# First layer of a hybrid block: the output product of six groups laid out with channels on the partitions and fed in split parts

## The reference, cut to what matters

```python
DIM, H, P, N = (256, 32, 64, 128)         # x: [1, 1024, 256]
proj = x @ Win.T                           # x_ssm, z: H*P each; B, C: H*N each; dt: H
dt = softplus(dt_raw + dt_bias)
xc, Bc, Cc = (silu(causal_conv(u, w)) for ...)     # 4 taps, per channel
decay = exp(dt * -exp(A_log)); dtx = dt[..., None] * xc
def step(h, inp):                          # one state of 64 x 128 for each head, zero at the start
    h = dec_t[..., None, None] * h + dtx_t[..., None] * B_t[:, :, None, :]
    y = jnp.einsum('bhpn,bhn->bhp', h, C_t)
y = y * rsqrt(mean(y * y, axis=-1) + 1e-06)        # norm over the 64 channels of a head
y = y * silu(z)
return y.reshape(B, T, H * P) @ Wout.T     # [1024, 2048] x [2048, 256]
```

## Time and profile before

| | us |
|---|---|
| median of 3 runs (1118.32 to 1120.6) | 1119.31 |
| the profiled execution | 1119.11 |
| its span, first to last instruction | 1117.8 |
| busy: PE | 1051.8 (94%) |
| busy: DVE | 779.3 (70%) |
| busy: POOL | 656.9 (59%) |
| busy: ACT | 595.8 (53%) |

### The profile page before, as it was taken

How to read it: one execution, slowest core, us unless ns; L and a number is a source line. 1 busy time by engine, 2 the same in 40 slices (tenths; PEclk the granted TensorE clock), 3 DMA queues, 4 the chain that set the end, 5 groups by cost and what they waited for, 6 DMA issues and landing times.

```text
span 1117.8 us, 24089 instructions
## 1 busy us (share of the span) xinstructions
PE 1051.8 (94%) x10046; PEld 875.9 (78%) x10046; DVE 779.3 (70%) x1177; ACT 595.8 (53%) x923; POOL 656.9 (59%) x651
## 2 busy tenths in 40 slices
PE   8899999999999999999989899998888879999998
PEld 6677788888888888888877788887654567788887
DVE  5679887888878888888857545555758853654554
ACT  5886787766677766777615222224954542423221
POOL 3967666677555776557653568554366452175553
PEclk9999999999999999999999999999999989999999
DMA  3322112111112121111200543302121120143321
GB/s 108 109 67 76 48 58 67 47 69 58 63 51 77 39 68 57 48 48 40 57 11 3 190 151 117 100 19 67 43 89 28 32 65 2 56 167 99 118 67 38
DMA packets 47217, 75.97 MB, mean 68 GB/s; under 512 B 11330, under 2 KB 34150, under 8 KB 47110
## 3 DMA queue, kind: packets, MB, share of 16 engines
q1 hardware_dynamic: 47110, 74.44, 20.8%
HBM read 68.13 MB, written 2.36 MB: 63 GB/s over the span
## 4 chain that ended last, share of the span: by engine, by line
PE 65%; DVE 17%; ACT 7%; POOL 5%; issue 4%; DMA 3%; SPq 0%; DVEq 0%; POOLq 0%; ACTq 0%
PE psum L654 33%; PE psum L877 8%; DVE arena L1581 6%; PE psum L742 5%; PE psum L626 4%; PE psum L784 4%; DVE arena L1618 3%; PE psum L734 2%; PE psum L986 2%; ACT arena L1166 1%; PE psum L950 1%; PE psum L1014 1%; DVE arena L1827 1%; DMA vT<-arena 1%; POOL arena L2034 1%
## 5 line engine op out<-in xcount | busy, mean ns | idle before, releaser
L654 PE MATMUL psum<-vT,split 128*128 128x512 f32 x2136 | 539.8, 402 | 12.9 <-DVE arena L1581 5.5
L654 PEld LDWEIGHTS psum<-vT,split 128*128 128x128 f32 x2136 | 391.6, 189 | 103.3 <-DVE arena L1581 7.5
L1581 DVE SCALAR_TENSOR_TENSOR arena<-psum,arena 128x1023 f32<-128x1023 f32 (+2 forms) x208 | 265.3, 1277 | 81.8 <-ACT arena L1166 65.5
L2007 POOL TENSOR_TENSOR split<-arena,split 128x256 fp32r<-128x256 f32 x178 | 132.9, 756 | 85.4 <-ACT split L1091 85.1
L1166 ACT ACTIVATE arena<-psum,arena 128x512 f32<-128x512 f32 x160 | 108.2, 691 | 137.5 <-PE psum L654 137.5
L2187 POOL TENSOR_TENSOR arena<-arena,bcast 128x512 f32<-128x512 f32 x64 | 84.6, 1324 | 113.3 <-ACT arena L1298 95.4
L1298 ACT ACTIVATE arena<-psum,arena 128x512 f32<-128x512 f32 x72 | 49.7, 690 | 173.6 <-PE psum L654 173.6
L1719 DVE SCALAR_TENSOR_TENSOR arena<-psum,arena 128x512 f32<-128x512 f32 x72 | 53.9, 749 | 123.0 <-POOL arena L2187 118.0
L877 PEld LDWEIGHTS psum<-split_down,split_hid 128*128 128x128 f32 x864 | 113.4, 192 | 10.2 <-DVE split_hid L1730 3.6
L877 PE MATMUL psum<-split_down,split_hid 128*128 128x256 f32 x864 | 116.2, 285 | 2.8 <-DVE split_hid L1730 2.8
L2034 POOL TENSOR_TENSOR arena<-arena,v 128x1021 f32<-128x1021 f32 x32 | 76.3, 2385 | 70.5 <-DVE arena L1581 70.5
(11 more groups left out here) (200 smaller groups left out, 1486.1 us busy)
## 6 DMA issues: line engine op xcount, KB each, us to landing
bcast<-scratch_a SPq DMA_DIRECT2D x32, 512.0 KB, 3.8
bcast<-scratch_e SPq DMA_DIRECT2D x32, 512.0 KB, 4.2
arena<-in_w_a SPq DMA_DIRECT2D x16, 768.0 KB, 4.4
arena<-in_wg SPq DMA_DIRECT2D x36, 128.0 KB, 3.6
arena<-in_wu SPq DMA_DIRECT2D x36, 128.0 KB, 3.5
arena<-in_wd SPq DMA_DIRECT2D x36, 128.0 KB, 3.9
arena<-in_wout_a SPq DMA_DIRECT2D x8, 256.0 KB, 4.5
vT<-arena SPq DMA_DIRECT2D x2, 1024.0 KB, 5.1
```

Source lines behind the costliest of these rows:

```text
L654: m = pe.matmul(bank, split[:, t % SPLITS, i, q, :], vT[:, j, q, half * BANK:(half + 1) * BANK], start=(n == 0), stop=(n == 3 * KD - 1))
L1581: dve.scalar_tensor_tensor(out=tile[:, s:T], in0=bank[:, 0:T - s], scalar=cw_a[:, j, i, TAPS - 1 - s:TAPS - s], in1=tile[:, s:T], op0=ALU. ...
L2007: pool.tensor_tensor(split[:, t % SPLITS, 1], raw, split[:, t % SPLITS, 0].bitcast(F32), ALU.subtract).then_inc(sem["split"], 1)
```

## The change

Groups 0 to 5: DVE's `gate` writes one buffer; ACT copies it as hi part (`gated_hi`), POOL subtracts to make the lo part (`gated_lo`), into `split_hid` (even pairs) or `split_gate` (odd pairs); Wout of the group is split in the same way (`wout_hi`, `wout_lo`). A unit of `project_out` is now 128 output channels by 512 tokens: six matmuls with 512 columns, Wout stationary. DVE adds units into `acc_a`, with channels on the partitions. Both late units come in odd pairs j, both early units in even pairs. In pair 15 `acc_a` is transposed back (units A) and added to x. Group 6 is multiplied in split parts after the loop (`last_split_out`, 48 matmuls with 256 columns), group 7 as before. `across` leaves out chunk 0, whose incoming state is zero; POOL sets that part of y to zero (`first_zero`). The last pair's squares, sums and norm go by heads. The buffers for gated y and Wout shrink; `experts` wait for `out_split` before they write `split_down` and `split_hid`.

```diff
+SUMMED = PAIRS // GROUP - 2
-def out_unit(j, late):
-    return [("O", (j - 3) // 2, 2 * (1 - j % 2) + late)] if j >= 3 else []
+def out_early(j):
+    if j == PAIRS - 1:
+        return [("A", 0), ("A", 1)]
+    return [("O", j // 2 - 2, 1, dh) for dh in range(2)] if j >= 4 and j % 2 == 0 else []
+def out_late(j):
+    if j == PAIRS - 1:
+        return [("A", 2), ("A", 3)]
+    return [("O", (j - 3) // 2, 0, dh) for dh in range(2)] if j >= 3 and j % 2 == 1 else []
...
@@ SP
-                        if g >= 2:
-                            on.wait_ge(sem["unit"], N_FILLED["O", g - 2, 3])
-                        load(f"wo{g % 2}", wout_a[:, g % 2], io["wout_a"][g])
+                        if g:
+                            on.wait_ge(sem["wo_lo"], g)
+                        load("wo0", wout_a, io["wout_a"][g])
@@ PE
-                    for c in range(NC):
+                    for c in range(1, NC):
                         m = by_halves(bank[:, c * PA:(c + 1) * PA], chunk(cv_a[:, j % 2, 3 + g, :], c),
...
+                        if unit[0] == "A":
+                            on.wait_ge(sem["dve_done"], N_DVE["O", SUMMED - 1, 1, 1])
+                            cs = (2 * unit[1], 2 * unit[1] + 1)
+                            transposes(unit, [chunk(acc_a[:, dh], c) for c in cs for dh in range(KD)])
+                            continue
+                        _, g, q, dh = unit
+                        on.wait_ge(sem["gated_lo"], GROUP * (g + 1))
+                        on.wait_ge(sem["wo_lo"], g + 1)
+                        for n, (i, (iw, ih)) in enumerate((i, p) for i in range(GROUP) for p in PRODUCTS):
+                            m = pe.matmul(bank, split_down[:, i, iw, dh * P:(dh + 1) * P], gated_parts(i)[:, ih, q],
+                                          start=(n == 0), stop=(n == 3 * GROUP - 1))
...
+                def last_split_out():
+                    on.wait_ge(sem["gated_lo"], GROUP * (SUMMED + 1))
+                    on.wait_ge(sem["wo_lo"], SUMMED + 1)
+                    for i in range(GROUP):
+                        for c in range(NC):
+                            for n, (iw, ih) in enumerate(PRODUCTS):
+                                m = pe.matmul(psum[:, c * D:(c + 1) * D],
+                                              gated_parts(i)[:, ih, c // 4, c % 4 * P:(c % 4 + 1) * P],
+                                              split_down[:, i, iw], ...)
+                    m.then_inc(sem["out_split"], 1)
...
-                    project_out(out_unit(j, 0))
+                    project_out(out_early(j))
...
-                    project_out(out_unit(j, 1))
+                    project_out(out_late(j))
...
-                project_out(out_unit(PAIRS, 0) + out_unit(PAIRS, 1))
+                last_split_out()
+                give_back(PAIRS - 1)
                 last_out(0)
-                give_back(PAIRS - 1)
                 last_out(1)
@@ ACT
+                def gated_hi(j):
+                    on.wait_ge(sem["dve_done"], N_DVE["F", j, 1])
+                    if j >= GROUP:
+                        on.wait_ge(sem["unit"], N_FILLED["O", j // GROUP - 1, 1, 1])
+                    act.copy(gated_parts(j)[:, 0], A["gated"].rearrange("p (q t) -> p q t", q=2)).then_inc(
+                        sem["gated_hi"], 1)
+                def wout_hi(g):
+                    act.copy(split_down[:, 0:GROUP, 0, :], wout_a).then_inc(sem["wo_hi"], 1)
...
                     turned(j, 1, 0)
+                    if j >= 3 and j % 2 == 1:
+                        gated_hi(j - 2)
                     project_to(1)
...
                     turned(j, 1, 1)
+                    if j >= 2 and j % 2 == 0:
+                        gated_hi(j - 2)
+                    if j >= 3 and j % 2 == 1:
+                        wout_hi((j - 3) // 2)
                     project_to(2)
@@ DVE
+                    _, g, q, dh = unit
+                    acc = acc_a[:, dh, q * BANK:(q + 1) * BANK]
                     if g:
+                        dve.tensor_tensor(acc, bank_of(unit), acc, ALU.add).then_inc(sem["dve_done"], 1)
+                    else:
+                        dve.tensor_copy(acc, bank_of(unit)).then_inc(sem["dve_done"], 1)
...
                     across(j, 0)
                     inside(j, 0)
+                    if j == PAIRS - 1:
+                        sum_squares_head(j, 0)
                     taps(4, 1)
-                    add_out(out_unit(j, 1))
+                    add_out(out_late(j))
@@ POOL
+                def first_zero(j):
+                    pool.memset(y_a[:, j % 2, 0, :], 0.0).then_inc(sem["y_zero"], 1)
+                def gated_lo(j):
+                    parts = gated_parts(j)
+                    on.wait_ge(sem["gated_hi"], j + 1)
+                    pool.tensor_tensor(parts[:, 1], A["gated"].rearrange("p (q t) -> p q t", q=2),
+                                       parts[:, 0].bitcast(F32), ALU.subtract).then_inc(sem["gated_lo"], 1)
...
                     carry_u(j, 1)
+                    first_zero(j)
                     project_to(1)
+                    if j >= 3 and j % 2 == 1:
+                        gated_lo(j - 2)
+                        wout_lo((j - 3) // 2)
                     if nxt < PAIRS:
                         light(nxt, 1)
                     project_to(2)
+                    if j >= 2 and j % 2 == 0:
+                        gated_lo(j - 2)
                     if j:
-                        normalize(j - 1)
+                        normalize(j - 1, (0, 1), j - 1)
...
-                normalize(PAIRS - 1)
+                for g in range(2):
+                    normalize(PAIRS - 1, (g,), PAIRS - 1 + g)
```

More of the change, by code:

```diff
@@ L313 @@
  gelu gated hid hid_hi hid_lo down down_hi down_lo ones_e router res x_out exp_step
- bconst cw_half fixed pad piece masked masked_p heads ud_b st_half tile_y y_out squared gates rms x_b x_a x_s sq_acc sq""".split()
+ bconst cw_half fixed pad piece masked masked_p y_zero gated_hi gated_lo wo_hi wo_lo out_split heads ud_b st_half tile_y y_out squared gates rms x_b x_a x_s sq_acc sq""".split()
 def hybrid_block(nc, io):
@@ L796, in last_out @@
+                def last_out(i):
+                    j = PAIRS - GROUP + i
+                    on.wait_ge(sem["dve_done"], N_DVE["F", j, 1])
+                    on.wait_ge(sem["wo0"], 16 * (PAIRS // GROUP))
                     for c in range(NC):
-                        m = pe.matmul(psum[:, c * D:(c + 1) * D], gated_a[:, g % 2, i, c * P:(c + 1) * P],
-                                      wout_a[:, g % 2, i, :], start=(i == 0 and c % 2 == 0), stop=(i == 1),
-                                      skip_group_check=True)
+                        m = pe.matmul(psum[:, c * D:(c + 1) * D], chunk(gated_of(j), c), wout_a[:, i, :],
+                                      start=False, stop=(i == 1), skip_group_check=True)
@@ L1646, in sum_squares, with sum_squares_head @@
                                           ALU.add).then_inc(sem["sq_sum"], 1)
+                def sum_squares_head(j, g):
+                    on.wait_ge(sem["square"], j + g + 1)
+                    on.wait_ge(sem["nrm"], 4 * (j - 1) + 1)
+                    dve.tensor_reduce(nrm_a[:, 0, g * NC:(g + 1) * NC],
+                                      y2.rearrange("p (c g m) -> p g c m", c=NC, g=2)[:, g], AX_X,
+                                      ALU.add).then_inc(sem["sq_sum"], 1)
                 def gate(j):
+                    if 0 < j < PAIRS - 1:
+                        on.wait_ge(sem["gated_lo"], j)
                     for q in range(2):
@@ L2060, in normalize @@
-                    for g in range(2):
+                    on.wait_ge(sem["nrm"], 4 * base + 4)
+                    for g in gs:
                         ys = y_a[:, j % 2, :, g * PA:(g + 1) * PA]
-                        pool.tensor_tensor(ys, ys, spread(n1[:, g * NC:(g + 1) * NC], PA), ALU.mult).then_inc(
+                        pool.tensor_tensor(ys, ys, spread(nrm_a[:, 1, g * NC:(g + 1) * NC], PA), ALU.mult).then_inc(
                             sem["normed"], 1)
+                def first_zero(j):
+                    if j >= 2:
+                        on.wait_ge(sem["unit"], N_FILLED["F", j - 2, 1])
+                    pool.memset(y_a[:, j % 2, 0, :], 0.0).then_inc(sem["y_zero"], 1)
```

113 lines of the change are left out of this document (65 added, 48 removed).

## The result

The changed kernel takes 1141.88 us (median of 4 runs, 1141.41 to 1143.82), the one before 1118.86 in the same rounds: a ratio of 1.0206 [1.0189, 1.0224]. It is slower, as forecast, but by 23.0 us where the sum had 15.7, and it lies 1.9 us above the range of 1120 to 1140. The profiled execution took 1141.41 us, with a span of 1140.1 (before 1117.8).

A forecast was written before the change was run, and what follows sets the result against it. It took two routes through the engines, not PE alone, as the bound: loop terms +2.5, +1.4 and +12.1, then +1.1 and -1.4 at the end, sum +15.7 on 1119.11 us, forecast 1135 us; range 1120 to 1140.

The forecast's parts named there:

- rival A: Whole kernel: PE is the bound and the rest follows, so the time falls by 13.7 to 1105 us; chance 0.12.
- B: Rival of no change: `gated_lo` hidden in POOL's gaps, `gated_hi` paid, about 1119.7 us; chance 0.06.
- C: Rival, slower still: copies at their upper bounds or the end's split product uncovered, 1141 us or above; chance 0.05.
- Even to odd 35.6: Distance between starts of head 0's masks, even to odd pair: route L's 32.63 + 2.36 + 0.6 us.
- Odd to even 35.43: Distance between starts of head 0's masks, odd to even pair: route S, 34.01 + 1.08 - 0.26 + 0.60 us.
- the ring: PE's and DVE's lists waiting on each other in the loop; route S through them took 34.01 us before.
- PE idle about 2 us ahead of `inside` in odd pairs: Sign expected in the profile after, with PE's busy share falling from 98% to about 93%.
- 14 to the copies: From pair 14's start of head 0's masks to pair 15's copies: 24.87 us for 23.74, +1.1.
- The end: From pair 15's copies to the last product: 25.4 us for 26.81, so -1.4, bounds -3.5 and +1.5.
- half a microsecond wide: Cover at the end: `last_split_out` ends on PE about 20.4 us after the copies, the norm at 21.
- route L: Light tiles' path through POOL, ACT and DVE between starts of head 0's masks: 32.63 us, 1.67 of room.
- route S: Scan's path from masks over `carry`, PE and ACT's term to DVE's taps: 34.01 us before the change.

The follow-up runs named there:

- e1: Changed kernel with POOL's `gated_lo` of even pairs moved behind `light(nxt, 3)` and the second exponents: 1127.99 us.
- b1: Kernel before the change with only `across` leaving out chunk 0 and `first_zero` added: 1116.16 us, ratio 0.9971.
- c3: Changed kernel with ACT's `gated_hi` of odd pairs moved behind the second turned copy: 1142.67 us.
- c1: Changed kernel with chunk 0 back in `across` and the last squares, sums and norm over both heads: 1143.72 us.
- e2: Changed kernel with four matmuls of ones on PE ahead of `inside` in odd pairs 3 to 13: 1135.97 us.
- e3: Changed kernel with three early units in an even pair and one late unit in an odd pair, for two and two: 1140.2 us.
- c2: Changed kernel with `gated_lo` behind the second exponents, three early units and one late, and four filling matmuls in odd pairs: 1122.33 us.
- d1: Kernel before the change with one unused 128x1024 fp32r subtraction added on POOL in even pairs, ahead of `normalize`: 1122.99 us.
- b3: Kernel before the change with `across` without chunk 0 and the last norm by heads, no split product: 1113.03 us, ratio 0.9944.

## Why the prediction was right and wrong

- **That it gets slower, and by which routes: right.** A copy of 2.36 us on an engine with 59% of the span cost about 2.1 us in each even pair (e1), since it lies on a route with little room; rival A, PE as the bound and a gain, fell. In the even pair PE is busy for 33.10 of 35.70 us, less than the 33.77 of before, and the pair is longer. The rule of the Trainium skill that was weighed there ("Perfetto Trace Analysis", section "Identifying the Most-Contended Engine") points the same way as A; this case's time did not go that way, 1141.88 us and not 1105. Work taken off PE did pay where it lay on the binding route: 0.24 us of 0.26 in each pair of b1. What the shares did not tell is the price of the work put on POOL. B fell too, as `gated_lo` was not hidden (e1). The time lies where C had put it, at 1141 or above, but neither of C's reasons came true: the copies cost 2.36 and 0.6, and the split product of the end was covered.
- **Even to odd 35.6: right**, 35.60 to 35.69, in both terms: 2.36 for `gated_lo` by its row, and 0.6 for `gated_hi` by c3.
- **Odd to even 35.43: right for the ring, 35.30.** The late unit 2.85 for 2.90, `across` 0.26 by c1. But only in two pairs of six.
- **The step that failed is what the prediction made of PE's idle time in odd pairs.** It foresaw it ("PE idle about 2 us ahead of `inside` in odd pairs") and counted it as a sign only, at no price beyond its length. The sum is made of durations at a granted clock of 1.00, which holds for every row of the loop before, whose idle time ahead of `inside` is 0.53. In the changed kernel, behind idle times of 2.03 to 2.06, the clock fell in four pairs at 1.5 us each (6.0), and once in the end of the layer (1.7). With 0.2 more from even to odd, less 0.7 at the start, 0.8 where odd to even was 0.13 under its forecast six times, and 0.6 in the rest of the end, this is what the layer has more than forecast: 21.5 for 15.7 (5.8). The other 1.5 of the 23.0 us are 0.8 in the second half and 0.7 between the profiled executions and the medians. e2 fills the idle time and changes nothing else: the falls in the loop are gone, and it measures 1136.
- **The range**: the bounds of the two copies gave 1128 to 1141, the stated range was 1120 to 1140, and neither had a bound for the clock. The bounds that it did have were wider than needed: 2.36 came out at 2.36.
- **14 to the copies: right**, 24.86 for 24.87. **The end: 25.4 forecast, 26.5 measured** (580.66 to about 607.2, the second half of the last product); without the slow `mix` it would be 24.8, and in c3, whose `mix` is not slow, it is about 25.0. The norm's 3.7 and the cover of the split product, "half a microsecond wide", were as said.
- **Not foreseen:** that a third early add brings route L above route S (e3, c2), and that d1's subtraction, with one tensor as both operands, is cheaper. The room of route L in the kernel before, 1.67, left out the one add; it did not enter the sum, since an odd pair of the changed kernel has no early add.

Open: why the clock falls in four of six places that look alike in the trace, with idle times of 2.03 to 2.06 us. No run here shows the choice, and the length of the idle time alone does not make it: 2.22 us in pair 2 of the changed kernel, 2.33 in c3's and 3.18 in c1's last pair were not followed by a fall. What is shown is that filling it ends the falls: none in e2 and c2, where 0.7 and 0.2 us are left.

## What to carry to other kernels

Price an added operation by the route through the engines that it lengthens and by the room of that route, not by how busy its engine is: 2.36 us on POOL at 59% cost 2.1, while 0.74 us a pair taken off PE at 94% made the loop no faster in any placement tried. Where a change opens idle time of some 2 us in front of matmuls on the binding route, add what the row of these matmuls would cost at half the clock, or fill the hole with work for TensorE and measure. When a change has several parts, measure each alone: here two parts of the three gain 0.56% together (b3), and the third alone loses 2.28% (c1), four times as much.

## What the runs showed of the hardware

- In the changed kernel's first layer an idle time of 2.03 to 2.06 us of TensorE was followed by work at 1.2 GHz in 5 places (4 odd pairs and the end; granted clock 0.53 over 3.25 us in pair 5), and by nothing in 2 (pairs 7 and 11). Idle times of 1.6 to 1.7 and one of 2.22 in its even pairs were not followed by it, one of 1.94 in c3 was. Idle times of 0.53 (before), and of 0.71 and 0.18 with 1.16 of work between them (e2), were never followed by one in the loop.
- A stretch at 1.2 GHz cost about 1.5 us from mark to mark where TensorE's list was on the binding route (odd pairs), and nothing where another route was (even pairs of c3, pair 2 of e3 and c1).
- Matmuls put into a hole only to fill it ended the falls in the loop, and the first layer ended at 602.90 and not at 608.12 us (medians, not of the same rounds, 1141.88 and 1135.97).
- POOL's subtraction over 128x1024 with an fp32r result takes 2.36 us from two different tensors and 1.85 with the same tensor, of zeros, twice (d1). Its power takes 1.67 us for 8 columns and 2.92 for 16.
